# A small MoE model on one core: second layer of block 1 token-major, two experts side by side

## What is computed

```python
# block 1, expert_ids from token ids, 4 experts, Wg = Wu = Wd = ctx
xn = layernorm(x)
for e in range(4):
    g = silu(xn @ ctx[e].T); u = xn @ ctx[e].T
    y = (g * u) @ ctx[e].T            # second layer, same matrix
    out = where(expert_ids == e, y, out)
x = x + out
# block 2
xn = layernorm(x)
scores = sigmoid(xn @ router_w.T)     # 16 experts, top 4 of scores + bias, weights normalised
x = x + sum_e combine[:, e] * ((silu(xn @ gate_e.T) * (xn @ up_e.T)) @ down_e.T) + shared(xn)
```

## Time and profile before

| | |
|---|---|
| median of 3 runs | 173.52 us (173.36 to 174.03) |
| the profiled execution | 173.89 us |
| its span, first to last instruction | 171.8 us |
| TensorE busy | 166.6 us, 97% |
| VectorE busy | 114.2 us, 66% |
| ScalarE busy | 67.8 us, 39% |
| GpSimd busy | 39.6 us, 23% |
| granted TensorE clock | 1.000 throughout |

### The profile page before, as it was taken

How to read it: one execution, slowest core, us unless ns; L and a number is a source line. 1 busy time by engine, 2 the same in 40 slices (tenths; PEclk the granted TensorE clock), 3 DMA queues, 4 the chain that set the end, 5 groups by cost and what they waited for, 6 DMA issues and landing times.

```text
span 171.8 us, 2194 instructions
## 1 busy us (share of the span) xinstructions
PE 166.6 (97%) x728; PEld 130.6 (76%) x728; DVE 114.2 (66%) x230; ACT 67.8 (39%) x112; POOL 39.6 (23%) x37
## 2 busy tenths in 40 slices
PE   6989999999999999999999999999999999999992
PEld 2568888888877888788787778788787887878881
DVE  0779778888984988588688528964744444444452
ACT  2472520551258254824664593152212222223320
POOL 2593000698200025539385000000000000000000
PEclk9999999999999999999999999999999999999999
DMA  4999000176400036742111200043361211100003
GB/s 137 307 373 352 23 4 2 25 236 227 122 0 4 15 130 181 203 160 67 61 61 61 61 0 4 8 126 126 113 195 45 75 65 61 62 0 4 2 0 122
DMA packets 7971, 16.41 MB, mean 95 GB/s; under 512 B 1336, under 2 KB 2200, under 8 KB 7832
## 3 DMA queue, kind: packets, MB, share of 16 engines
q1 hardware_dynamic: 7960, 16.27, 29.0%
HBM read 15.08 MB, written 1.18 MB: 95 GB/s over the span
## 4 chain that ended last, share of the span: by engine, by line
PE 97%; ACT 0%; POOL 0%; DVE 0%; issue 0%; DVEq 0%; POOLq 0%
PE bank L853 26%; PE bank L913 14%; PE bank L911 13%; PE bank L912 13%; PE bank L931 7%; PE bank L934 7%; PE bank L932 7%; PE bank L943 4%; PE bank L820 2%; PE bank L907 1%; PE bank L908 1%; PE bank L832 1%; ACT xn_hi L433 0%; POOL warm L383 0%; DVE xt L732 0%
## 5 line engine op out<-in xcount | busy, mean ns | idle before, releaser
L913 PE MATMUL bank<-xn_lo,gu_hi 128*128 128x512 f32 (+1 forms) x104 | 41.0, 394 | 0.0
L911 PE MATMUL bank<-xn_hi,gu_lo 128*128 128x512 f32 x96 | 37.9, 395 | 0.0
L912 PE MATMUL bank<-xn_hi,gu_hi 128*128 128x512 f32 x96 | 37.8, 394 | 0.0
L501 ACT ACTIVATE h_hi<-hid 128x512 fp32r<-128x512 f32 (+1 forms) x26 | 16.4, 632 | 45.7 <-DVE hid L720 45.7
L725 DVE TENSOR_TENSOR h_lo<-hid,h_hi 128x512 fp32r<-128x512 f32 (+1 forms) x26 | 20.2, 778 | 15.6 <-ACT h_hi L501 15.6
L913 PEld LDWEIGHTS bank<-xn_lo,gu_hi 128*128 128x128 f32 (+1 forms) x104 | 19.4, 186 | 5.0
L491 ACT ACTIVATE act_sb<-bank 128x512 f32<-128x512 f32 (+1 forms) x26 | 15.4, 594 | 18.1 <-PE bank L913 18.0
L398 POOL TENSOR_TENSOR gu_lo<-stage,gu_hi 128x512 fp32r<-128x512 f32 x12 | 17.9, 1516 | 17.6 <-ACT gu_hi L426 17.6
L912 PEld LDWEIGHTS bank<-xn_hi,gu_hi 128*128 128x128 f32 x96 | 18.0, 187 | 4.4
L911 PEld LDWEIGHTS bank<-xn_hi,gu_lo 128*128 128x128 f32 x96 | 18.0, 187 | 4.4
L931 PE MATMUL bank<-h_hi,wd_lo 128*128 128x512 f32 (+1 forms) x52 | 20.6, 396 | 0.0
(11 more groups left out here) (76 smaller groups left out, 213.1 us busy)
## 6 DMA issues: line engine op xcount, KB each, us to landing
stage<-gu_d SPq DMA_DIRECT2D x6, 512.0 KB, 3.5
stage<-wd_d SPq DMA_DIRECT2D x3, 512.0 KB, 4.1
x<-comb_d SPq DMA_DIRECT2D x8, 192.0 KB, 2.7
ids<-comb_d SPq DMA_DIRECT2D x8, 192.0 KB, 3.0
stage<-ctx_d SPq DMA_DIRECT2D x4, 256.0 KB, 5.0
xt<-xt_d SPq DMA_DIRECT2D x1, 1024.0 KB, 10.3
x<-comb_d SPq DMA_DIRECT2D x8, 128.0 KB, 3.1
ids<-comb_d SPq DMA_DIRECT2D x8, 128.0 KB, 2.8
```

The lines of the kernel that those rows point to most:

```text
L911: nc.tensor.matmul(out[:], gu_lo[:, cols], xn_hi[:, h, k], start=(k == 0), stop=False)
L912: nc.tensor.matmul(out[:], gu_hi[:, cols], xn_hi[:, h, k], start=False, stop=False)
L913: ins = nc.tensor.matmul(out[0:rows, :], gu_hi[:, wide], xn_lo[:, h, k], start=False, stop=(k == KC - 1))
```

## The change

The second layer of block 1 becomes token-major. A tile is 128 tokens: the hidden tokens are the stationary operand, and the weights of two experts, 2 x 256 columns, the moving one, so that a tile is 2 pairs x 2 chunks x 3 = 12 matmuls of 512 columns into two banks. VectorE picks with a mask of one column per tile, broadcast along 256 features (`owned`), and adds x in place, so that x1 is where the second norm reads it: the x1 transposes, `add_block_1`, `copy_x1` and the load of xt go. All four first-layer mixes stand first, then the eight tiles, with item 0's gate and up between tiles 5 and 6. The second norm of half 0 is done in two groups of two tiles. Tokens are dealt to tiles in blocks of 32, so that VectorE's stream transpose of 32x32 blocks can turn x1 to feature-major for the output: `turn_x1` at items 5 and 11 (`X1_TURNS`) writes xt, SP sends it to DRAM in eight writes (`write_x1`) and reads it back into place an item later (`read_x1`). Spread rows now go to ids and, from item 3 on, to ctx_lo, since x is kept. The core of the diff:

```diff
-X1_AT = 2
+BLOCKS = D // LANES
+X1_TURNS = (5, 11)
...
-BY_VECTOR = ((0, 2), (0, 2), (0, 1), (0, 2))
+BY_VECTOR = ((0, 2), (0, 2), (0, 2), (0, 2))
+NORM_GROUPS = [(0, (0, 1)), (0, (2, 3)), (1, (0, 1, 2, 3)), (2, (0, 1)), (2, (2, 3)), (3, (0, 1, 2, 3))]
...
         def spread(n):
 
             if n % SPREADS < 2:
-                return x[:, 0:TT].rearrange("p t d -> p (t d)")[:, n % SPREADS * HALF:(n % SPREADS + 1) * HALF]
-            return ids[:, (n % SPREADS - 2) * HALF:(n % SPREADS - 1) * HALF].bitcast(F32)
+                return ids[:, n % SPREADS * HALF:(n % SPREADS + 1) * HALF].bitcast(F32)
+            return ctx_lo[:, n % SPREADS - 2].rearrange("p k d -> p (k d)").bitcast(F32)
...
+            def write_x1(h):
+                sp.wait_ge(x1_turned, (h + 1) * TT)
+                by_block = x1_d[h].rearrange("(b j) (q c) -> b q j c", b=BLOCKS, c=P)
+                blocks = xt[:, h].rearrange("p k c -> p (k c)")
+                for b in range(BLOCKS):
+                    sp.dma_start(by_block[b], blocks[:, b * P:(b + 1) * P]).then_inc(x1_out, 16)
+
+            def read_x1(h):
+                sp.wait_ge(x1_out, (h + 1) * BLOCKS * 16)
+                sp.dma_start(xt[:, h], x1_d[h].rearrange("(k f) c -> f k c", k=KC)).then_inc(xt_in, 16)
...
                     spread_rows(g)
                 if g in (4, 6):
                     load_piece(len(pieces) - 2 + (g == 6))
+                if g in X1_TURNS:
+                    write_x1(X1_TURNS.index(g))
+                if g - 1 in X1_TURNS:
+                    read_x1(X1_TURNS.index(g - 1))
...
+            first_z(("mix", 2))
             high_part(4)
             high_part(5)
+            silu_z(2)
+            first_z(("mix", 3))
             high_part(6)
-            first_z(4)
             high_part(7)
+            silu_z(3)
...
+            def tile(j, masked):
+
+                u = ("tile", j)
+                z = prod[:, turn[u] % 2, 0:D]
+                dve.wait_ge(z_first, turn[u] + 1)
+                dve.wait_ge(dstep, masked)
+                for e in range(1, E1):
+                    dve.wait_ge(z_done, z_at[u, e // 2])
+                    if e > 1:
+                        dve.wait_ge(z_picked, picks_of(u, e - 1))
+                    nc.vector.copy_predicated(z, owned[:, e - 1, j:j + 1].to_broadcast([P, D]),
+                                              ring_bank(u, e // 2)[:, e % 2 * D:(e % 2 + 1) * D]).then_inc(z_picked, 1)
+                dve.wait_ge(z_picked, picks_of(u, E1 - 1))
+                nc.vector.tensor_tensor(x[:, j], z, x[:, j], ALU.add).then_inc(x1_done, 1)
+
+            def turn_x1(h):
+
+                for t in range(TT):
+                    nc.vector.transpose(x1_blocks[h][:, t], x[:, h * TT + t].rearrange("p (b i) -> p b i", i=LANES)).then_inc(x1_turned, 1)
...
                 if g == 5:
-                    layer_norm_apply(3)
+                    layer_norm_apply(5)
+                if g in X1_TURNS:
+                    turn_x1(X1_TURNS.index(g))
             output(1)
...
-            for n in range(2, 5):
-                mix(n)
-            mix(5, {1: lambda: (x1_transposes(0, 0), x1_transposes(0, 1))})
-            mix(6, features=[0])
-            norm_transposes("n2", 2, 0)
-            mix(6, experts=[0, 1], features=[1])
+            mix(2)
+            mix(3)
+            for j in range(TT + 1):
+                tile(j)
+            tile(TT + 1, {0: lambda: norm_transposes("n2", 2, 0)})
             gate_or_up(0, False)
             gate_or_up(0, True)
-            mix(6, experts=[2, 3], features=[1])
-            mix(7)
+            tile(6)
+            tile(7)
```

More of the change, by code:

```diff
@@ L612, in thresholds, with owners, pick @@
                 return last
-            def pick(n, masked, experts=range(1, E1)):
-                h = mixes[n][1]
-                dve.wait_ge(z_first, n + 1)
+            def owners():
+                dve.wait_ge(owner_in, 16)
+                for e in range(1, E1):
+                    last = step(nc.vector.tensor_scalar(owned[:, e - 1], owner[:], float(e * PER_EXPERT), None, ALU.is_ge))
+                return last
+            def pick(b, masked, experts=range(1, E1)):
+                u = ("mix", b)
+                h, _ = mixes[b]
+                dve.wait_ge(z_first, turn[u] + 1)
```

402 lines of the change are left out of this document (202 added, 200 removed).

## The result

The changed kernel takes **203.27 us** (median of 4, 201.88 to 204.50) beside 173.78 us (173.36 to 174.16) for the kernel before on the same chip: 1.170 times as long, 95% interval 1.160 to 1.179. The forecast was 188.5 us with a range to 194: the sign was right, the loss, 29.5 us, twice as large as the 15 forecast. The profiled execution took 204.17 us, 202.4 of them in the span.

The account below looks back on a forecast made before the run. TensorE, busy 97% of its span, was taken as the bound: 173.5 - 1.75 (transposes) + 3.0 (front) + 6.7 and 6.0 (round trip, two halves) + 1.0 (clock) = 188.5 us. Range 181.5 to 194 us.

Parts of the forecast that it names:

- the transposes' 1.75 us: On TensorE: removing sixteen transposes of x1, two batches of eight at 0.87 us, saves 1.75 us, all on the path.
- the places of all stalls: TensorE would idle ahead of the second norm's first transposes, item 8's up, item 9's gate and item 14's up projection.
- the order in SP's queue: SP issues item 6's rows only after waiting for the transposes and issuing eight writes; VectorE's gap 7.9 us.
- Front of block 2: Ahead of the second norm's transposes: VectorE's smaller instructions and meetings with GpSimd make TensorE wait +3.0 us, bounds 0.8 and 5.
- 1.1 for the thresholds and 0.8 for the additions: In block 2's front: the us VectorE loses where its thresholds and third and fourth tiles' additions meet GpSimd's work.
- Round trip, first half: Items 6 to 9: VectorE waits for rows queued behind x1's writes, making TensorE late by +6.7 us, bounds 3.5 and 9.
- From the second issue to landing 2.8: Within the round trip's gap: item 6's spread rows land 2.8 us after their second DMA issue, bounds 1.9 to 4.1.
- the read back of x1 [...]: nothing: In SP's queue: reading x1 back costs nothing, since the output needs it some 30 us later.
- Second half: Items 12 to 14: the same gap delays the hidden product that item 14's up projection needs, +6.0 us, bounds 3 and 8.5.
- The clock: TensorE's clock falling in long stalls costs zero to 2.3 us each, the second hidden; +1.0 us taken in all.
- rival (d): The clock falls in two or three stalls, unhidden: 1 to 4.6 us above the clock term, 190 to 195 us; chance 0.14.
- The tile matmuls come at another pitch than 0.2335: Sign of a wrong prediction: block 1's second-layer tile matmuls were assumed 0.2335 us each; another pitch would move the sum.

Follow-up runs that it names:

- trip_alone: Kernel before with only x1's round trip added: four stream transposes at items 5 and 11, eight writes and read back, own buffer; 195.34 us, ratio 1.124.
- front_fixed: turns_late plus second-half thresholds made on GpSimd in its idle stretch and GpSimd's low parts reordered; 176.47 us.
- pool_light: Changed kernel with GpSimd's low parts of five early weight pieces made over 8 columns only, the rest zero; 198.25 us.
- front_more: front_fixed with the three owner masks of 8 columns also made on GpSimd in its idle stretch; 174.64 us, ratio 1.004.
- quarter_bytes: Changed kernel with each of the eight writes of x1, and the read back, cut to a quarter of its partitions and bytes; 198.70 us.
- read_late: Changed kernel with only the read back of x1 issued three items later; 201.94 us.
- filler_long: Changed kernel with 42 small warm-up matmuls between gate and up of item 14, where TensorE otherwise stands idle; 202.48 us.
- after_last: Changed kernel with its owner and owned tensors placed last in SBUF, same instructions; the changed kernel's shorter pitch is worth 1.3 us against it.
- before_pad: Kernel before with two unused small tensors (32 and 24 bytes a partition) ahead of the statistics; two executions near 171 us, two near 176.
- pad128: Kernel before with one unused tensor of 128 bytes a partition ahead of the statistics; 171.9 us.
- filler: Changed kernel with 30 small warm-up matmuls between gate and up of item 14, where TensorE otherwise stands idle; 202.58 us.
- turns_late: Changed kernel with x1 transposed back at items 9 and 17, SP's writes three items and its reads four items later; 181.01 us.

## Why the prediction was right or wrong

**Right.** TensorE as the bound of the kernel before, no gain but the transposes' 1.75 us (1.7), the places of all stalls, a transpose of x1 of 0.37 each (four in 1.41), a write's issue of 0.575 (0.57), the copies of 256 columns (three in 1.54 with their gap, 1.6 forecast), the order in SP's queue as the largest cause. trip_alone, on its own, came out at 195.3 us where its expectation had 195 to 198.

**Front of block 2, +3.0, measured +8.5.** The step that failed is the price of meeting GpSimd. The sum had 1.1 for the thresholds and 0.8 for the additions, 1.9; it took the one stretched low part of the earlier trace rows, 0.85 us, as the scale for all, and did not add such a low part itself, which now stands ahead of the third mix. Measured were 0.84 for that low part, 2.2 for the thresholds, 2.3 for one addition and 2.1 for shift and tile, 7.4 in all. Even an operation on 2 columns, the shift, took 1.21 us in place of 0.15. The price is not set by VectorE's instruction but by how long GpSimd's low part lasts; three masks of 8 columns beside two low parts took 2.50 us in place of 0.30 (front_fixed). pool_light, front_fixed and front_more show it by taking meetings away.

**Round trip, first half, +6.7, measured +11.8.** Two steps failed. "From the second issue to landing 2.8" was 5.1: in the kernel before no writes of x1 are ahead of these rows, here 512 KB of them are, and smaller writes bring it down to 3.7 (quarter_bytes). And "the read back of x1 [...]: nothing" was wrong: not its transfer costs, but SP's wait for the writes, with item 7's rows behind it. read_late takes it away, and with it VectorE's 2.48 us and TensorE's 2.45. The rest of the difference, 5.1 - 2.3 - 2.45 = 0.35 us, no run explains.

**Second half, +6.0, measured +7.3.** Again the landing: the gap is 9.12 us against 7.9, and from the second issue at about 139.5 to VectorE's product at 143.43 it is 3.9 against 2.8. The term is 1.3 too small, and 1.2 of that is the gap.

**The clock, +1.0, measured 6.8 us of slow matmuls.** The rival (d), 1 to 4.6 us more, was the case, and it was beyond even its upper end. The step that failed is the size and the number of the falls. The term had zero to 2.3 us for each long stall, one of them hidden, and took 1.0 us in all; the clock fell behind four waits, 1.25 to 2.2 us each, one of the waits only 2.45 us long. Whether VectorE hides a fall stays open. By the Trainium skill ("TensorE: Matmul & The Clock Gate", the gate's oscillation) an array that idles between bursts pays for each return; the trace agrees, with 5 to 11 matmuls at 0.43 us each time. How much of the 6.8 is real loss, and not hidden by other waits, was estimated for one fall only, with filler_long: 2.1 of 2.2.

**The pitch, taken as unchanged, measured -3.9.** "The tile matmuls come at another pitch than 0.2335" stood among what would make the prediction wrong. They did, but with all the others, and for a reason outside the change's idea: the two small tensors for the owners moved what lies behind them by 64 bytes. By TensorE's account it hid 3.9 us of the loss; by the time of after_last it was 1.3.

With the 1.7 us that no term explains, the account is 173.5 - 1.75 + 8.5 + 11.8 + 7.3 + 6.8 - 3.9 + 1.7 = 203.9 us. The largest misses are the clock's term by 5.8 us, the front's by 5.5 and the first round trip's by 5.1.

**Where it ends.** Once the transposes back stand in slack, SP's order keeps rows ahead of writes, and GpSimd keeps off, front_more is near the kernel before, 174.64 beside 173.68 us. But it has the shorter pitch, and the kernel before has that too with padding alone. On equal placement, 64 bytes, and at a granted clock of 1.00, front_more takes 173.4 to 173.5 us and before_pad 170.6 to 171.1: the change still loses 2.3 to 2.9 us. pad128 is the fastest version whose times all agree, 171.9 us.

## What to carry to other kernels

Before moving a wait in a DMA-issuing queue, list what is queued behind each wait in it, the wait for a read back included, and price a landing with the writes that are under way at that time. Price a VectorE instruction on SBUF beside a wide GpSimd pass, such as the low parts here, by the GpSimd pass's length, however small the instruction is. And when adding a tensor, compare the matmul pitch of the unchanged stages before crediting or blaming the change.

## What was not expected of the hardware

The start-to-start time of fp32 matmuls of 512 columns takes one of several values between 0.2268 and 0.2336 us by the placement of SBUF tensors alone, the same in each kernel that has the placement. And the clock also fell behind short idle times: 2.32 us in filler, and in front_more 0.70 and 0.87 us with a few matmuls between, behind which they came 0.43 us apart. Start, us and idle time in that kernel's timeline of TensorE:

```profile
94.30 0.47 PE L962 MATMUL bank<-xn_hi,gu_hi 128*128 128x512 f32 x1 [0.70 <-ACT xn_hi L476]
94.61 0.40 PE L963 MATMUL bank<-xn_hi,gu_lo 128*96 128x512 f32 x1
95.87 0.51 PE L968 MATMUL bank<-xn_lo,gu_hi 128*128 128x512 f32 x1 [0.87 <-DVE xn_lo L642]
...
97.51 0.63 PE L963 MATMUL bank<-xn_hi,gu_lo 128*96 128x512 f32 x1
97.94 0.63 PE L968 MATMUL bank<-xn_lo,gu_hi 128*96 128x512 f32 x1
```

In turns_late, with 0.26 and 0.87 us of idle time at the same place, the clock did not fall. Of front_more's ten executions the three with a granted clock of 1.00 took 173.4 to 173.5 us, and the seven at 0.98 to 0.99 took 174.1 to 176.6, so its spread goes with the granted clock; only one of the ten was profiled.
